# Third attention layer: parts stored once, four part buffers, first head loaded inside the preparation; first layer's division behind its loop

## The reference, cut to what matters

```python
x = L0_attn_x
x = x + layernorm(L0_attn(layernorm(x)))
x = x + layernorm(L0_ffn(layernorm(x)))      # then L1, L2, L3 likewise

def L0_attn(x):                              # first layer
    q, k, v = heads(x @ w_qkv.T)
    s = einsum('bhqd,bhkd->bhqk', q, k) * scale + bias(rel_bias_table)[h, q, k]
    o = einsum('bhqk,bhkd->bhqd', softmax(s), v)
    return merge(o) @ w_proj.T + b_proj

def L2_attn(x):                              # third attention layer
    q, k, v = heads(x @ w_qkv.T); q = q * scale
    rp = clip(j - i, -31, 31) + 31           # 63 distances
    s = einsum('bhid,bhjd->bhij', q, k)
    s += take(einsum('bhid,hdm->bhim', q, rpe_k_table), rp)
    s += take(einsum('bhjd,hdm->bhjm', k * scale, rpe_q_table), rp).T
    a = softmax(s)
    o = einsum('bhij,bhjd->bhid', a, v)
    S = segment_sum(a over j, by rp)         # probability per distance
    o += einsum('inbh,hnd->bhid', S, rpe_v_table)
    return merge(o) @ w_proj.T + b_proj
```

## Time and profile before

| | |
|---|---|
| median of 3 runs | 2282.48 us (2277.91 to 2284.94) |
| profiled execution: time, span | 2282.85 us, 2281.1 us |
| granted TensorE clock, mean | 0.89 |
| busy over the span: PE, DVE, ACT, POOL | 79%, 74%, 47%, 37% |
| mean busy share of the 16 DMA engines by the main queue | 18.6% |
| first layer; third attention layer, in the span | 0 to 351 us; 1302 to 1834 us |

### The profile page before, as it was taken

One profiled execution on the slowest core, in us unless ns is written; L12 is line 12 of the kernel. 1 busy time (PEld: TensorE's weight loads), 2 busy tenths in 40 slices (PEclk: granted clock), 3 DMA queues, 4 the chain that ended last, 5 costly groups with the idle time before them and its releaser, 6 DMA issues. The chain is left out here.

```text
span 2281.1 us, 46344 instructions
## 1 busy us (share of the span) xinstructions
PE 1797.6 (79%) x16408; PEld 1307.2 (57%) x16408; DVE 1682.7 (74%) x4004; ACT 1077.9 (47%) x2023; POOL 839.1 (37%) x632
## 2 busy tenths in 40 slices
PE   6999983888888975499999666887888659997656
PEld 3776661555555653367777544555555348886444
DVE  5999987776666757779999854998989772224674
ACT  5888862555545531144444234565555323332532
POOL 3000006765555501134434344455544218911111
PEclk8999996999999997689999877999888769998887
DMA  3111102100000000100000074454444250000000
GB/s 116 50 54 48 45 16 72 34 18 18 17 18 18 17 1 5 25 7 18 24 23 12 12 229 123 147 159 150 144 155 140 76 211 21 19 0 7 1 1 22
DMA packets 130614, 129.42 MB, mean 57 GB/s; under 512 B 76565, under 2 KB 107131, under 8 KB 129682
## 3 DMA queue, kind: packets, MB, share of 16 engines
q1 hardware_dynamic: 129522, 126.78, 18.6%
q10 hardware_dynamic: 928, 0.47, 0.1%
HBM read 78.59 MB, written 40.81 MB: 52 GB/s over the span
## 5 line engine op out<-in xcount | busy, mean ns | idle before, releaser
L2814 ACT ACTIVATE l2a_pr<-l2a_ps_s,l2a_nm 128x512 f32<-128x512 f32 x256 | 173.9, 685 | 142.1 <-DVE l2a_nm L2737 139.3
L518 ACT ACTIVATE l0a_pr<-l0a_sm,l0a_nm 128x512 f32<-128x512 f32 x256 | 185.1, 724 | 58.8 <-DVE l0a_nm L396 51.0
L396 DVE CUSTOM_DVE_ANT_0 l0a_sm<-l0a_ps_s,l0a_tb 128x512 f32<-128x512 f32 x256 | 174.9, 684 | 22.3 <-PE l0a_ps_s L602 15.5
L1692 POOL TENSOR_TENSOR l1f_h<-l1f_lm,l1f_sg 128x512 f32<-128x512 f32 x72 | 92.6, 1286 | 184.8 <-DVE l1f_lm L1756 184.8
L2737 DVE TENSOR_REDUCE l2a_nm<-l2a_ps_s 128x2 f32<-128x1024 f32 x128 | 156.7, 1224 | 4.4
L2744 DVE STREAM_TRANSPOSE l2a_tt<-l2a_pr 128x1024 f32<-128x1024 f32 x128 | 158.0, 1234 | 0.6 <-ACT l2a_pr L2814 0.6
L610 PE MATMUL l0a_ps_p<-top_c_ident,l0a_pr 128*128 128x128 f32 x1024 | 155.6, 274 | 0.0
L610 PEld LDWEIGHTS l0a_ps_p<-top_c_ident,l0a_pr 128*128 128x128 f32 x1024 | 128.9, 142 | 21.9 <-issue 0.9
L1818 ACT ACTIVATE l1f_csb<-l1f_ps_c,l1f_b3e 128x512 f32<-128x512 f32 x128 | 88.2, 689 | 107.5 <-PE l1f_ps_c L1604 107.2
L2071 ACT ACTIVATE l2f_h<-l2f_ps_h 128x512 f32<-128x512 f32 x128 | 76.6, 599 | 131.6 <-PE l2f_ps_h L1604 125.4
L2038 DVE SCALAR_TENSOR_TENSOR l2f_acc<-l2f_ps_y,l2f_comb,l2f_acc 128x128 f32<-128x128 f32 x112 | 31.6, 345 | 133.1 <-PE l2f_ps_y L2112 133.0
(11 more groups left out here) (534 smaller groups left out, 5131.6 us busy)
## 6 DMA issues: line engine op xcount, KB each, us to landing
l_qband<-l2a_staged SPq DMA_DIRECT2D x16, 768.0 KB, 15.9
l2a_qb<-l_qband SPq DMA_DIRECT2D x16, 768.0 KB
l2a_sb<-l_pband SPq DMA_DIRECT2D x32, 384.0 KB
l0a_tb<-l_bias SPq DMA_DIRECT2D x16, 448.0 KB
l2a_ks<-l_k SPq DMA_DIRECT2D x16, 384.0 KB
l_pband<-l2a_pr SPq DMA_DIRECT2D x32, 192.0 KB, 8.0
l_pband<-l2a_pr SPq DMA_DIRECT2D x32, 144.0 KB, 2.5
l2f_upw<-in_L_ffn_up_weights SPq DMA_DIRECT2D x9, 512.0 KB, 11.2
```

What stands on the lines that cost most here:

```text
L396: v.tensor_tensor_reduce(sm[j % 4][:, :], ps_s[j % 2][:, :], tb[slot][:, off:off + N][:, ::-1], -1.0, 3e38, ALU.add, ALU.min, nm[:, j % 4: ...
L518: a.activation(pr[j % 4][:, :], sm[j % 4][:, :], ACT.Exp, bias=nm[:, j % 4:j % 4 + 1], scale=-1.0).then_inc(m["p_ready"], 1)
L2814: a.activation(pr[slot][:, 2 * (g % 2) + u, :], ps_s[g % 2][:, u, :], ACT.Exp, bias=nm[:, g % 2, u:u + 1], accum_out=rs[:, n % 2, 2 * (g % ...
```

## The change

In the first layer `normalize` becomes `keep`: one copy of the 36 columns (8 outputs and the sum, four tiles) from PSUM to a tile `ro` that has room for all heads; the reciprocal and the multiply for all heads of a batch are done by `divide(b)`, in the tail behind the loop, and PE's projection waits for each batch by itself.

In the third layer the scratch holds each part once, in the first layer's layout, so a batch has 1 store for q and 1 for each key variant; `parts` has four buffers, and semaphores of their own count the `k32`, q and k stores. ACT's order in the preparation is written out anew, DVE's spread of the value table moves from batch 0 to batch 2, the zero stores are spread over the batches, and the loads of ones and zeros come first. The tiles `qs`, `ks`, `rawk`, `kshift` and the first `qb` are made ahead of the preparation, and head 0's raw keys, shifts, parts, bias rows and band are loaded there, and expanded on POOL. Every head's parts are loaded with `load_parts`, so a head has 7 loads in place of 3.

```diff
-L0_TR_LAG, L0_EVAC_LAG, L0_PV_LAG, L0_OC_LAG, L0_OT_LAG, L0_NORM_LAG = 3, 4, 6, 7, 8, 9
+L0_TR_LAG, L0_EVAC_LAG, L0_PV_LAG, L0_OC_LAG, L0_OT_LAG, L0_KEEP_LAG = 3, 4, 6, 7, 8, 9
+DIVIDE_AT = [2 * UNITS + 1, 2 * UNITS + 3, 2 * UNITS + 5]
...
-                def normalize(g, b, h):
-
-                    r, o = rd[:, b % 2, :].unsqueeze(2), ps_q[b % 2].rearrange("p (t w) -> p t w", w=VW)
+                def keep(g, b, h):
+
+                    o = ps_q[b % 2].rearrange("p (t w) -> p t w", w=VW)
                     v.wait_ge(m["ot_ps"], g + 1)
-                    v.reciprocal(r, o[:, :, HD:HD + 1]).then_inc(m["pool"], 1)
-                    v.wait_ge(m["pool"], g + 1)
-                    v.tensor_tensor(ao[:, b * NT:(b + 1) * NT, bass.ds(h * HD, HD)], o[:, :, 0:HD],
-                                    r.broadcast_to([P, NT, HD]), ALU.mult).then_inc(m["o_done"], 1)
+                    v.tensor_copy(ro[:, b * NT:(b + 1) * NT, bass.ds(h * (HD + 1), HD + 1)], o[:, :, 0:HD + 1]).then_inc(m["o_done"], 1)
+
+                def divide(b):
+
+                    rows = slice(b * NT, (b + 1) * NT)
+                    o = ro[:, rows, :].rearrange("p t (h e) -> p t h e", e=HD + 1)
+                    v.wait_ge(m["o_done"], HEADS * B - B + b + 1)
+                    v.reciprocal(rd[:, rows, :].unsqueeze(3), o[:, :, :, HD:HD + 1]).then_inc(m["pool"], 1)
+                    v.wait_ge(m["pool"], b + 1)
+                    v.tensor_tensor(ao[:, rows, :].rearrange("p t (h e) -> p t h e", e=HD), o[:, :, :, 0:HD],
+                                    rd[:, rows, :].unsqueeze(3).broadcast_to([P, NT, HEADS, HD]), ALU.mult).then_inc(m["ao_ready"], 1)
...
-                for j in range(2 * UNITS, 2 * UNITS + L0_NORM_LAG):
+                for j in range(2 * UNITS, 2 * UNITS + L0_KEEP_LAG):
                     if j < 2 * UNITS + L0_EVAC_LAG:
                         evac_step(j, HEADS // 2 - 1, False)
                     late(j, HEADS // 2 - 1, False)
+                    if j in DIVIDE_AT:
+                        divide(DIVIDE_AT.index(j))
+                divide(B - 1)
...
-                pe.wait_ge(m["o_done"], HEADS * B)
                 for b in range(B + 1):
                     if b < B:
+                        pe.wait_ge(m["ao_ready"], b + 1)
...
-    return {"q3": nc.dram_tensor("l2_q3", (P, len(Q_PARTS), T * P), BF16).ap(),
-            "k3": nc.dram_tensor("l2_k3", (P, len(K_PARTS), 2, T * P), BF16).ap(),
+    return {"q3": nc.dram_tensor("l2_q3", (3, P, T * P), BF16).ap(),
+            "k3": nc.dram_tensor("l2_k3", (3, P, 2 * T * P), BF16).ap(),
...
-        HEAD_LOADS = 3
-        STORES = 1 + 3 + 2 * 3
+        HEAD_LOADS = 2 * len(PART_RUNS) + 1
+        ONCE_LOADS = 3
...
-            parts = p.sb("parts", [P, 2, 3, 3, N], BF16)
+            parts = p.sb("parts", [P, B, 3, 3, N], BF16)
...
                     sp.wait_ge(m["q_lo"], b + 1)
-                    for first, count, part in Q_ROW_RUNS:
-                        sp.dma_start(q3[:, first:first + count, cols], parts[:, b % 2, 0, part:part + 1, :].broadcast_to([P, count, N])).then_inc(stored[b % 2], 16)
+                    sp.dma_start(q3.rearrange("c p t -> p c t")[:, :, cols], parts[:, b, 0, :, :]).then_inc(m["q3_stored"], 16)
                     for v in range(2):
                         sp.wait_ge(m["lo_ready"], 2 * b + v + 1)
-                        for first, count in K_ROW_RUNS:
-                            sp.dma_start(k3[:, first:first + count, v, cols], parts[:, b % 2, v + 1, 0:count, :]).then_inc(stored[b % 2], 16)
+                        sp.dma_start(k3.rearrange("c p t -> p c t")[:, :, v * T * P + b * N:v * T * P + (b + 1) * N],
+                                     parts[:, b, v + 1, :, :]).then_inc(m["k3_stored"], 16)
+                for i in range(2):
+                    sp.wait_ge(k32_stored[i], 16 * (B // 2))
+                sp.wait_ge(m["tab_stored"], 16)
+                load_raw_keys(sp, 0)
+                load_shifts(sp, 0)
                 sp.wait_ge(m["g_lo"], 1)
...
+                sp.wait_ge(m["q3_stored"], 16 * B)
+                load_parts(sp, qs[0], q3, 0, head_loaded[0], True)
+                sp.wait_ge(m["k3_stored"], 16 * 2 * B)
+                load_parts(sp, ks[0][:, :, :].rearrange("p v t -> p (v t)"), k3, 0, head_loaded[0], False)
                 sp.wait_ge(m["g_stored"], 16 * B)
+                load_bias_rows(sp, 0)
                 sp.wait_ge(m["zeroed"], 16 * (QBAND_RING + 2 * PBAND_RING))
                 sp.wait_ge(m["l_ready"], ROUND["q", 0, 3])
                 sp.dma_start(qband[0][:, 0:ROW], staged[0][:, :, :].rearrange("p a n -> p (a n)")).then_inc(q_stored[0], 16)
+                sp.wait_ge(m["rvd_ready"], B)
+                sp.dma_start(rv_d.rearrange("h p n -> p h n"), rvd[:, :, :, :].rearrange("p h k n -> p h (k n)")).then_inc(m["rvd_stored"], 16)
+                sp.wait_ge(q_stored[0], 16)
+                sp.dma_start(qb[0][:, :, :].rearrange("p a n -> p (a n)"), skewed(qband[0], GRP - 1, -1, ROW)).then_inc(qband_read[0], 16)
+                sp.wait_ge(m["rvd_stored"], 16)
...
-                        if b >= 2 and v == 1:
-                            g.wait_ge(stored[b % 2], 16 * STORES * (b // 2))
...
+                expand(g, 0)
...
-                        a.wait_ge(stored[b % 2], 16 * STORES * (b // 2))
+                        a.wait_ge(k32_stored[b % 2], 16 * (b // 2))
...
+                copy_z(0)
+                copy_z(1)
+                a.wait_ge(m["t_loaded"], 32)
+                bases(0)
+                copy_z(2)
+                copy_z(3)
+                highs(0)
+                for b in range(1, B):
+                    bases(b)
+                    highs(b)
...
-                    sp.dma_start(q[0:KROWS, :], q3[h * HD:(h + 1) * HD].rearrange("d c t -> (d c) t")).then_inc(sem, 16)
-                    sp.dma_start(k[0:KROWS, :, :].rearrange("p v t -> p (v t)"),
-                                 k3[h * HD:(h + 1) * HD].rearrange("d c v t -> (d c) (v t)")).then_inc(sem, 16)
...
+                    load_parts(sp, qs[h % 2], q3, h, head_loaded[h % 2], True)
+                    load_parts(sp, ks[h % 2][:, :, :].rearrange("p v t -> p (v t)"), k3, h, head_loaded[h % 2], False)
+                    load_bias_rows(sp, h)
```

More of the change, by code:

```diff
@@ L258, in l0_attn @@
         pT = [s.sb(f"pT{i}", [P, N]) for i in range(RING)]
[L259 removed]
+        rd = s.sb("rd", [P, T, HEADS])
+        ro = s.sb("ro", [P, T, HEADS * (HD + 1)])
         ao = s.sb("ao", [P, T, D])
@@ L2240, in l2_attn @@
         xk = s.sb("xk", [P, GRP + T * P + GRP + HALF])
+        qs = [s.sb(f"qs{i}", [L2_ROWS, T * P], BF16) for i in range(2)]
+        ks = [s.sb(f"ks{i}", [L2_ROWS, 2, T * P], BF16) for i in range(2)]
+        rawk = [s.sb(f"rawk{i}", [P, T * P // HALF]) for i in range(2)]
+        kshift = [s.sb(f"kshift{i}", [P, WINDOW_COLS]) for i in range(2)]
+        qb = [s.sb("qb0", [P, NB, BAND])]
         ps_s = [s.ps(f"ps_s{i}", [P, 2, N]) for i in range(2)]
@@ L2260, in l2_attn @@
         q_stored = [m["qw0"], m["qw1"], m["qw2"]]
-        stored = [m["st0"], m["st1"]]
-        HEAD_LOADS = 3
-        STORES = 1 + 3 + 2 * 3
+        k32_stored = [m["k32_st0"], m["k32_st1"]]
+        HEAD_LOADS = 2 * len(PART_RUNS) + 1
+        ONCE_LOADS = 3
         ROUND = band_order()
@@ L2269, in p_stores, with load_raw_keys, load_shifts, load_bias_rows @@
             return 16 * sum(1 if i % 4 in (1, 2) else 2 for i in range(o % PR_RING, o + 1, PR_RING))
+        def load_raw_keys(sp, h):
+            each = T * P // HALF
+            src = bass.AP(k32.tensor, k32.offset + h * HD * T * P, [[each, HALF], [T * P, HD], [1, each]])
+            sp.dma_start(rawk[h % 2][:, :], src).then_inc(keys_loaded[h % 2], 16)
+        def load_shifts(sp, h):
+            src = bass.AP(rel_d.tensor, rel_d.offset + h * HD * KEY_SHIFTS, [[1, HALF], [KEY_SHIFTS, HD], [1, WINDOW_COLS]])
+            sp.dma_start(kshift[h % 2][:, :], src).then_inc(shifts_loaded[h % 2], 16)
+        def load_bias_rows(sp, h):
+            src = bass.AP(g3.tensor, g3.offset + h * 3 * T * P, [[T * P, 3], [HEADS * 3 * T * P, 2], [1, T * P]])
+            sp.dma_start(ks[h % 2][KROWS:FROWS, :, :], src).then_inc(head_loaded[h % 2], 16)
+        def skewed(band, offset, step, width):
+            pitch = width + GRP
+            return bass.AP(band.tensor, band.offset + offset, [[GRP * pitch, B], [pitch + step, GRP], [1, width]])
+        def expand(g, h):
+            g.wait_ge(keys_loaded[h % 2], 16 * (h // 2 + 1))
+            if h:
+                g.wait_ge(m["l_ps"], ROUND["k", h - 1, KEY_ROUNDS - 1])
+            g.tensor_tensor(xk[:, GRP:GRP + T * P].rearrange("p (g c) -> p g c", c=HALF), rawk[h % 2][:, :].unsqueeze(2).broadcast_to([P, T * P // HALF, HALF]),
+                            own_shift.unsqueeze(1).broadcast_to([P, T * P // HALF, HALF]), ALU.mult).then_inc(m["xk_ready"], 1)
         chained = [0]
@@ L2448, in _ @@
                         if i == 0:
```

(15 more changed lines are left out.)

120 lines of the change are left out of this document (49 added, 71 removed).

## The result

| | before | changed |
|---|---|---|
| median (runs) | 2283.71 us (4, 2277.91 to 2288.13) | 2347.43 us (4, 2345.13 to 2354.89) |
| ratio, 95% interval | | 1.0285 (1.0262 to 1.0309) |
| profiled execution: time, span | 2282.85, 2281.1 | 2354.89, 2353.3 |
| granted TensorE clock, mean | 0.89 | 0.872 |

The change made the kernel 64 us slower; 50 were forecast (2333, range 2292 to 2385). The busy shares of the page say little: the engines do the same work in a longer span (TensorE 12 us more, at a lower clock).

What follows compares the result with a forecast made beforehand. DVE and the four DMA lanes carrying the band loads were taken to bound the third layer's loop together, DVE alone the first's. 2282.85 - 23 - 6.5 + 80 = 2333 us, range 2292 to 2385.

Steps and rivals of the forecast that it cites:

- division behind the first loop: First layer's loop: a copy replaces reciprocal, wait and multiply per group; -23 us (-32 to -11).
- preparation: Third layer's preparation: fewer stores, head 0 loaded early; net -6.5 us (-11 to +2).
- head loads in the loop: Third layer's loop: narrower loads heap 6.75 us on a full lane; 5.75 more per head, 14 heads, +80 us.
- 4.47 - 0.39 = 4.08: First layer's loop: TensorE's floor per group in us, from the period less its wait for the output copy.
- I end the block 1.5 later: Third layer's preparation: block end 1.5 us later, from 5 earlier against 8 longer, partly beside each other.
- The 5 earlier: Third layer's preparation: without ScalarE's store waits, the chain to the last bias part shortens by about 5 us.
- 8 longer: Third layer's preparation: head 0's parts put 204 KB on the lowest lane, 8 us ahead of the block's last stores.
- SP is waiting for landings ..., which hides it: Third layer's loop: SP's 5.8 us of waiting per head hides 2.7 us for issuing four more transfers.
- The loads cost nothing: Rival, third layer's loop: heads keep their 26.0 us period, only gains remain; 2253 us, 7%.
- A chain on top of the lane: Rival, third layer's loop: SP's issuing adds to the lane's work, 9.45 us per head, 132 in all; 2385 us, 13%.
- Gains at their best, cost at its least: Rival, whole kernel: gains of 32 and 11 us, head loads costing 55; 2295 us, 10%.
- The first loop gives nothing back: Rival, first layer's loop: TensorE takes DVE's place at once; 2356 us, inside the forecast's range, no chance of its own.

Runs made afterwards that it cites:

- 1: Kernel before with only the first layer's part of the change: 2263.18 us, ratio 0.9928.
- 6: Changed kernel with the first layer's 36-column copy made twice per group, the second into an unread tile: one run, output copies span 262.5 us.
- 12: Changed kernel, bands by batch, head loads over eight lanes, relative-value store before head 0's loads, first band's wait and load behind the block's end: 2220.43 us, ratio 0.9727.
- 2: Changed kernel with the same six part transfers per head spread over eight lanes, dimension outermost: 2285.9 us.
- 3: Changed kernel with each band load split by batch into four 32-row transfers on sixteen lanes, head loads as changed: 2233.54 us, ratio to before 0.9786.
- 5: Changed kernel with parts stored repeatedly and each head's 48 q and k rows loaded in six 16-row transfers: 2305.53 us.
- 7: Changed kernel with head loads issued two of SP's steps earlier, transfers as changed: 2347.17 us.
- 10: Kernel before with band loads split by batch over sixteen lanes, nothing of the change: 2243.19 us, ratio 0.9816.
- 11: Changed kernel with band loads split by batch and part transfers with the dimension outermost: 2226.43 us, ratio 0.9743.
- 4: Changed kernel with parts stored repeatedly again and the old two 48-row loads per head: 2272.23 us.
- 8: Changed kernel with repeated rows in six 16-row transfers, head loads issued two of SP's steps earlier: 2315.8 us.

## Why the prediction came out as it did

| step | predicted | profiled execution | shown by |
|---|---|---|---|
| division behind the first loop | -23 | -16.0 | output copies 278.4 to 262.4; 1, 6 |
| preparation | -6.5 | -2.0, of it 2 scatter | first exponential 93.4 to 91.4; 1, 12 |
| head loads in the loop | +80 | +84.0 | (31.93 - 25.93) x 14, from head 1 on; 2, 3, 5, 7 |
| head 0 to head 1 | 0 | +5.9 | 33.6 - 27.7, TensorE's clock; 6 |
| sum | +50.5 | +71.9 | spans 2281.1 to 2353.3 |

**What bounds the kernel** was right: take the bands off the four lanes and the period falls to 24.4 to 24.6 whatever the head loads look like (3, 10, 11), with DVE at 97% in experiment 3. DMA share alone would have said there was room: it is 0.37 in the slowest loop and 0.55 in the fast one.

**Division.** The mechanism held, DVE handing over to TensorE, and the size was off. The failing number is "4.47 - 0.39 = 4.08" as TensorE's floor. Both parts were single rows: over all groups the distance was 278.4/63 = 4.42, and TensorE's floor is 262.4/63 = 4.165. The 4.165 is what the loop takes now that TensorE sets it. The copy's price (0.10, taken as 0.20) does not matter, as experiment 6 shows: even two hide.

**Preparation.** The step that failed is "I end the block 1.5 later": it ended 6.9 later. The 5 earlier came out (4.6 for the band's store); the "8 longer" was too small, and nothing of it hid: from the band's store to the block's end it is 12.3 us in place of 0.7, 11.5 longer. The band's store is queued behind head 0's loads, SP waits for it inside the block (1340.62 to 1349.77), and what TensorE has to do for head 0's keys starts only behind the block. So the forecast's wait of 8.85 for head 0's load did go, and came back as the block's end. Experiment 2 gives back 4 us by head 0's loads on more lanes, 12 another 6.7 by moving the waits.

**Head loads.** The mechanism was right, and the rows bear it: three lanes, then two, with all engines waiting, where the earlier trace rows had shown it in the first layer. The Trainium skill ("DMA: Bandwidth & Descriptors", section "Why a DMA increments its semaphore by 16 and not by 1") gives the count of engines as the largest number up to 16 that divides the slowest dimension of both patterns, and the lowest-numbered ones; the shares 0.19 and 0.14 agree with counts of three and two, and that these are the lanes of the bands is shown by experiment 3, where the wait goes with the bands.

The row of head 1's first products separates the loop into head 0 and the rest. Changed kernel, kernel before, and experiment 6, which has the changed kernel's head loads and its head 0 from 1368.6:

```profile
L2916 PE MATMUL l2a_ps_s<-l2a_ks,l2a_qs x4: 208/221/234, 1404.2 to 1405.1; 65*32 65x32 bf16 x4
L2876 PE MATMUL l2a_ps_s<-l2a_ks,l2a_qs x4: 176/190/190, 1416.1 to 1416.1; 65*32 65x32 bf16 x4
L2918 PE MATMUL l2a_ps_s<-l2a_ks,l2a_qs x4: 176/190/190, 1397.7 to 1397.8; 65*32 65x32 bf16 x4
```

From head 1 on heads are (1851.2 - 1404.2)/14 = 31.93 apart, 25.93 before: 6.00 where 5.75 was forecast, 84.0 us in 14 intervals. Head 0 takes 33.6 us in place of 27.7, but only 29.1 in experiment 6 with the same loads, so these 5.9 us are not theirs; they come from TensorE's clock (last section). They may be the larger part of the 8 us by which the profiled pair differs more than the medians; the other executions have no trace to tell.

The budget of a lane comes out too. Bands: 9 x 768 KB and 18 x 384 KB in the 300 us, 14.2 MB, at 102 GB/s for the four 139 us, 0.463 of each; the other work is 0.37 - 0.463/4 = 0.254. At 31.93 us a head that is 14.8 + 8.1, and for the parts that the lowest lane has above the mean 6.75, as predicted: 29.6 us, with 2.3 of pause. Predicted were 30.2 and 1.5. Both budgets count the band loads issued in 300 us, 11 and 9, and leave out a part of a head; with one head's 1.57 MB, 15.4 us a lane in either kernel, they are some 24.0 of 25.9 and 30.1 of 31.9, an estimate, and the pause, 1.9 and 1.8, hardly shrank. (The low end of this term, 50, comes out at 45 from its own numbers: 22.5 + 6.75 - 26.0 = 3.2, x 14. Nothing hangs on it here.)

One thing in it was wrong all the same: "SP is waiting for landings ..., which hides it". The number of transfers is not free on full lanes. By experiments 4, 5 and the changed kernel, from head 1 on, the 6.03 us between 25.90 and 31.93 are 2.75 for four more transfers on balanced lanes and 3.28 for heaping them up; the forecast had 5.75 for the heap alone. The lane budget and this split don't agree. That the price of a transfer is smaller when its packets run on few lanes is possible and not tested, so how much of the changed kernel's 6 us is which stays open. The sum agrees better than its parts deserve, and that is luck.

**Rivals.** "The loads cost nothing" fell, but would have been right on free lanes (experiment 3). "A chain on top of the lane" fell as a sum (+84, not 132), while its ingredient, the price of four more transfers, is real at 2.75 us on balanced lanes. "Gains at their best, cost at its least" (2295) fell with both halves: less gained, and more paid than its 55. "The first loop gives nothing back" fell (experiment 1).

## What to carry to other kernels

Ask of each transfer on how many DMA engines it runs, and look at a window in which it runs alone: a mean share of 0.48 hid four full lanes, and splitting the narrow loads into four of 32 rows each, with these rows outermost, was worth 41 us in the kernel before, more than anything in the change. A layout that saves stores once and makes every load narrower is paid for in every turn of the loop. And work moved into a preparation is only gained if the block's end doesn't wait for it.

## What had not been expected of the hardware

With lanes that are behind, a transfer has a price beyond its bytes: four more per head, rows and lanes unchanged, cost 2.75 us, 0.69 each (experiments 4 and 5, from head 1 on), and issuing them earlier does not give it back (8). On free lanes four more cost nothing that shows (experiments 10 and 11: 24.43 both).

SP can be held in an issue while lanes are behind: a load of queries took it 6.87 us at the longest in the changed kernel, where the median is 0.69, and at most 0.78 with the bands on sixteen lanes (experiment 3). Issued earlier, the load goes through and the next issues are held (experiment 7).

The granted clock follows the wait: 0.50 (1.2 GHz) in the windows shown from 1591, while TensorE is idle, and still after its return at 1595; over the loop 0.83 in place of 0.89. And it can stay low with TensorE busy. Behind the preparation the clock is 0.50 in every kernel here; in the changed kernel's profile it still is from 1390 to 1404, with TensorE busy all the time, while experiment 6 does the same 122 products of head 0 in 9 us at 0.99:

```profile
1390.00:1404.00 14.00, 14.00 (x122) 10.15 (x115) 11.74 (x15) 7.95 (x22) 8.57 (x4) 0.50 0.38 121
1388.00:1397.00 9.00, 8.13 (x122) 5.87 (x115) 8.90 (x11) 6.77 (x19) 7.42 (x4) 0.99 0.48 147
```

Head 0 is 4.5 us longer by it (33.6 against 29.1). Why the clock rose later in one execution than in the other, these runs don't show.
